# Ids as columns of the first load, bias computed first, base weights of chunk 0 requested ahead of chunk 1

## The chip, the cores and the metric

The kernel runs on one core of a Trainium2 chip. The time is that of the device in microseconds, for one execution. It stands beside the span of a profiled execution, which is the stretch from the first to the last recorded instruction. The engines are PE (TensorE, matrix products), ACT (ScalarE), DVE (VectorE), POOL (GpSimd) and SP (which issues transfers here). PE's weight loads have a row of their own, PEld.

## The reference: a dense layer, two of eight low-rank experts and a residual

`x` has 64 sequences of 32 tokens with 512 features, all in fp32, and each sequence has one id from 0 to 7. Cut to what is computed:

```python
base = einsum('btd,od->bto', x, W)                       # 512 x 512
logits = einsum('btd,ed->bte', x, Wr) + 5.0 * one_hot(id, 8)
topw, topi = top_k(logits, 2)
gates = sum(one_hot(topi, 8) * softmax(topw)[..., None]) # 8 gates for each token, 6 of them zero
h = einsum('btd,erd->bter', x, A)                        # 8 experts, rank 16
lora = einsum('bter,bte,eor->bto', h, gates, B)
out = x + base + 2.0 * lora
```

## The kernel before

**Tiles.** The 2048 tokens make 16 tiles of 128, and partition p holds tokens 16p to 16p + 15, so that each partition belongs to one sequence (two partitions to each of the 64). The 512 features make four chunks of 128 (KC = 4), over which the products sum. A tile has two groups of output columns: *heads*, 392 of them (output columns 256 to 511, the 128 columns of `A`, the 8 logits), and *base*, 256 (output columns 0 to 255). Each group has a PSUM bank for each of three slots, and tile t uses slot t mod 3.

**Three products for one.** For accuracy each fp32 operand is split into a rounded upper part (fp32r) and the rest: `x_hi` and `x_lo`, `w_hi` and `w_lo`, `b_hi` and `b_lo`. A product is then three matmuls, hi by hi (n = 0), `x_hi` by `w_lo` (n = 1) and `x_lo` by `w_hi` (n = 2). ACT makes `x_hi` (L221 for tiles 0 and 1, L231 later), `w_hi` (L224) and `b_hi` (L254). POOL subtracts for `x_lo` (L210, L205). DVE subtracts for `w_lo` (L342) and `b_lo` (L358), and makes `w_hi` of the heads columns of chunk 0 itself (L346).

**The opening.** The host packs the transposed x of tiles 0 and 1 and all the weights into `in_first`, chunk by chunk: 256 columns of x, 392 heads columns, 256 base columns. SP issues x of chunk 0 (L163), then chunks 1, 2 and 3 whole (L165, 452 KB each), then x of tile 2, `b`, and groups of three tiles. ACT issues the heads weights (L242, 196 KB) and then the base weights of chunk 0 (L243, 128 KB). POOL issues the ids (L195), broadcast from 64 numbers to 128 partitions. While these travel, PE runs nine matmuls on constants (L466). Then it goes through tiles 0 and 1 together, chunk by chunk, with a wait in front of each part of a chunk (L469 to L507): for `x_hi`, for `w_hi`, for `x_lo`, for `w_lo`. The last chunk waits for all four and then does heads for both tiles, then base.

**Gates.** As soon as the heads of a tile are done, DVE reads the logits, adds `bias` (L284), finds the two best (L289, L292), builds the gates (L301 to L306, with one exponential on ACT, L239) and writes the gated 128 columns to `gh` (L313). PE transposes `gh` (L424), ACT and DVE split the result (L235, L278), and PE adds its product with `b` into the two banks (`lora`, L433 and L437). DVE adds x and writes the output (L323, L328). For tile 0 the transpose stands on PE behind the first six heads products of tile 2 (L510 to L512).

**Order.** Every engine has its own hand-written order, with semaphores between them. On DVE that of the opening is: cast of the heads weights (L346), `w_lo` of chunk 0's heads, `w_lo` of chunk 0's base and of chunks 1 to 3 (L349 to L351), `bias` (L354, which waits for the ids), `b_lo` (L358), and then the gates of tile 0. On ACT: x of chunk 0, base weights of chunk 0, then x and all weights of each chunk (L248 to L251), x of tile 2, `b`. On POOL: the ids, the identity matrix, the numbers 0 to 7 (`expert`, L198), then `x_lo` of chunks 0 to 3, of tile 2, of tile 3 and so on. Behind tile 3 all engines run loops in steps of one tile.

Of the kernel before, what the change touches and what calls it, by code (L numbers as in the profile page):

```python
# [7 lines left out]
I32 = mybir.dt.int32  # L8
# [22 lines left out]

FIRST = (0, 1)
FIRST_X = len(FIRST) * P
GROUPS = 4
GROUPED = GROUPS * SLOTS


def cond_resid_program(nc: bass.Bass, first: bass.AP, xT: bass.AP, x: bass.AP, ids: bass.AP,
                       b: bass.AP, out: bass.AP):


# [8 lines left out]
    with ctx:  # L50
        def sb(name, shape, dt=FP32):
            return ctx.enter_context(nc.sbuf_tensor(name, shape, dt))
# [4 lines left out]
        def sem(name):  # L57
            return ctx.enter_context(nc.semaphore(name))


        first_sb = sb("first_sb", [P, KC, FIRST_X + WIDTH])
        xT_sb = sb("xT_sb", [P, TILES - len(FIRST), KC * P])
        x_sb = sb("x_sb", [P, TILES, D])
        out_sb = sb("out_sb", [P, TILES, O])
# [2 lines left out]
        b_sb = sb("b_sb", [ER, O])  # L67
        b_hi = sb("b_hi", [ER, O], FP32R)
        b_lo = sb("b_lo", [ER, O], FP32R)
        ids_sb = sb("ids_sb", [P, 1], I32)  # L70
        expert = sb("expert", [P, E], I32)
        bias = sb("bias", [P, E])
        ident = sb("ident", [P, P])
# [30 lines left out]
        wb_landed = sem("wb_landed")  # L104
        chunk_landed = [sem(f"chunk_landed{k}") for k in range(1, KC)]
        b_landed = sem("b_landed")
        ids_landed = sem("ids_landed")
        out_stored = sem("out_stored")

        ident_zeroed = sem("ident_zeroed")  # L110
# [33 lines left out]
        heads_cols, base_cols, all_cols = slice(0, HEADS), slice(HEADS, WIDTH), slice(0, WIDTH)  # L144
        chunks = [slice(k * P, (k + 1) * P) for k in range(KC)]
        first_x = [first_sb[:, k, 0:FIRST_X].rearrange("p (t c) -> p t c", c=P) for k in range(KC)]
        w_sb = first_sb[:, :, FIRST_X:FIRST_X + WIDTH]
        w = first[:, :, FIRST_X:FIRST_X + WIDTH]

        block = ctx.enter_context(nc.Block())  # L150

        @block.sync
        def _(sp):
            def load(dst, src, t, n, landed):
                sp.dma_start(dst[:, bass.ds(t, n), :], src[:, bass.ds(t, n), :]).then_inc(landed, 16)

            def store(t, n):
                sp.dma_start(out[:, bass.ds(t, n), :], out_sb[:, bass.ds(t, n), :]).then_inc(out_stored, 16)

            def load_xT(t, n, landed):  # L160
                load(xT_sb, xT, t - len(FIRST), n, landed)

            sp.dma_start(first_sb[:, 0, 0:FIRST_X], first[:, 0, 0:FIRST_X]).then_inc(x_landed, 16)  # L163
            for k in range(1, KC):
                sp.dma_start(first_sb[:, k, :], first[:, k, :]).then_inc(chunk_landed[k - 1], 16)  # L165
            load_xT(2, 1, xT_third)
            sp.dma_start(b_sb[:, :], b).then_inc(b_landed, 16)
# [12 lines left out]
            with sp.Fori(0, GROUPS) as g:  # L180
                sp.wait_ge(out_made, SLOTS * g + SLOTS)
                store(SLOTS * g, SLOTS)
            for t in range(GROUPED, TILES - 1):
                sp.wait_ge(out_made, t + 1)
                store(t, 1)

            sp.wait_ge(heads_read, TILES)
            sp.dma_start(out[:, TILES - 1, BASE:O], out_sb[:, TILES - 1, BASE:O]).then_inc(out_stored, 16)
            sp.wait_ge(out_made, TILES)
            sp.dma_start(out[:, TILES - 1, 0:BASE], out_sb[:, TILES - 1, 0:BASE]).then_inc(out_stored, 16)  # L190
            sp.wait_ge(out_stored, 16 * (GROUPS + TILES - 1 - GROUPED + 2))

        @block.gpsimd
        def _(pool):
            pool.dma_start(ids_sb[:, :], ids.rearrange("(s a) o -> s a o", a=1)  # L195
                           .to_broadcast([SEQS, P // SEQS, 1])).then_inc(ids_landed, 16)
            nc.gpsimd.memset(ident[:, :], 0.0).then_inc(ident_zeroed, 1)
            nc.gpsimd.iota(expert[:, :], pattern=[[1, E]], base=0, channel_multiplier=0).then_inc(expert_made, 1)  # L198
            pool.wait_ge(ident_zeroed, 1)
            nc.gpsimd.affine_select(out=ident[:, :], in_=ident[:, :], compare_op=ALU.not_equal, fill=1.0, base=0,  # L200
                                    pattern=[[-1, P]], channel_multiplier=1).then_inc(ident_made, 1)

            def x_lower(t, s):
                pool.wait_ge(x_hi_made, t - 1)
                nc.gpsimd.tensor_tensor(x_lo[:, s, :], xT_sb[:, t - len(FIRST), :], x_hi[:, s, :].bitcast(FP32),  # L205
                                        ALU.subtract).then_inc(x_lo_made, 1)

            for k in range(KC):
                pool.wait_ge(chunk_hi_made, k + 1)
                nc.gpsimd.tensor_tensor(x_lo[:, 0:2, chunks[k]], first_x[k],  # L210
                                        x_hi[:, 0:2, chunks[k]].bitcast(FP32), ALU.subtract).then_inc(chunk_lo_made, 1)
            with pool.Fori(0, GROUPS) as g:
                for j in range(2, 2 + SLOTS):
                    x_lower(SLOTS * g + j, j % SLOTS)
            for t in range(2 + GROUPED, TILES):
                x_lower(t, t % SLOTS)

        @block.scalar
        def _(act):
# [3 lines left out]
            def w_upper(k, cols):  # L223
                nc.scalar.activation(w_hi[:, k, cols], w_sb[:, k, cols], ACT.Copy).then_inc(w_hi_made, 1)  # L224
# [15 lines left out]
                                     bias=top[:, 1:2]).then_inc(e2_made, 1)  # L240

            act.dma_start(w_sb[:, 0, heads_cols], w[:, 0, heads_cols]).then_inc(wh_landed, 16)  # L242
            act.dma_start(w_sb[:, 0, base_cols], w[:, 0, base_cols]).then_inc(wb_landed, 16)  # L243
            act.wait_ge(x_landed, 16)
            chunk_upper(0)
            act.wait_ge(wb_landed, 16)
# [1 line left out]
            for k in range(1, KC):  # L248
                act.wait_ge(chunk_landed[k - 1], 16)
                chunk_upper(k)  # L250
                w_upper(k, all_cols)  # L251
            x_upper(2, 2, xT_third, 16)
            act.wait_ge(b_landed, 16)
            nc.scalar.activation(b_hi[:, :], b_sb[:, :], ACT.Copy, scale=SCALING).then_inc(b_hi_made, 1)  # L254
# [20 lines left out]
        def _(dve):  # L275
# [65 lines left out]
            def w_lower(k, cols):  # L341
                nc.vector.tensor_tensor(w_lo[:, k, cols], w_sb[:, k, cols], w_hi[:, k, cols].bitcast(FP32),  # L342
                                        ALU.subtract).then_inc(w_lo_made, 1)

            dve.wait_ge(wh_landed, 16)
            nc.vector.tensor_copy(w_hi[:, 0, heads_cols], w_sb[:, 0, heads_cols]).then_inc(wh_hi_made, 1)  # L346
            dve.wait_ge(wh_hi_made, 1)
            w_lower(0, heads_cols)
            for k in range(KC):  # L349
                dve.wait_ge(w_hi_made, k + 1)  # L350
                w_lower(k, all_cols if k else base_cols)  # L351
            dve.wait_ge(expert_made, 1)
            dve.wait_ge(ids_landed, 16)
            nc.vector.tensor_scalar(bias[:, :], expert[:, :], ids_sb[:, :], LANG_BIAS, ALU.is_equal,  # L354
                                    ALU.mult).then_inc(bias_made, 1)
            dve.wait_ge(bias_made, 1)
            dve.wait_ge(b_hi_made, 1)
            nc.vector.scalar_tensor_tensor(b_lo[:, :], b_sb[:, :], SCALING, b_hi[:, :].bitcast(FP32), ALU.mult,  # L358
                                           ALU.subtract).then_inc(b_lo_made, 1)
# [36 lines left out]
        def _(pe):  # L396
# [7 lines left out]
            def heads_product(s, k, n):  # L404
                return product(heads_ps[s][:, 0:HEADS], s, heads_cols, k, n)
# [67 lines left out]
            pe.wait_ge(w_hi_made, 1)  # L473
            for t in FIRST:
                base_product(t, 0, 0)
            pe.wait_ge(w_lo_made, 1)
            for t in FIRST:
                heads_product(t, 0, 1)
            pe.wait_ge(chunk_lo_made, 1)
            for t in FIRST:  # L480
                heads_product(t, 0, 2)
                base_product(t, 0, 2)
            pe.wait_ge(w_lo_made, 2)
            for t in FIRST:
                base_product(t, 0, 1)
            for k in range(1, KC - 1):
                pe.wait_ge(chunk_hi_made, k + 1)
                pe.wait_ge(w_hi_made, k + 1)
                for t in FIRST:
                    heads_product(t, k, 0)  # L490
                    base_product(t, k, 0)
                pe.wait_ge(chunk_lo_made, k + 1)
                for t in FIRST:
                    heads_product(t, k, 2)
                    base_product(t, k, 2)
                pe.wait_ge(w_lo_made, k + 2)
                for t in FIRST:
                    heads_product(t, k, 1)
                    base_product(t, k, 1)
            pe.wait_ge(chunk_hi_made, KC)  # L500
            pe.wait_ge(w_hi_made, KC)
            pe.wait_ge(chunk_lo_made, KC)
            pe.wait_ge(w_lo_made, KC + 1)
            for t in FIRST:
# [67 lines left out]
```

## Time and profile before

| | us |
|---|---|
| median of 3 runs (lowest, highest) | 82.12 (82.05, 82.36) |
| profiled execution, its own time | 82.09 |
| its span | 80.3 |
| PE busy | 75.4 |
| DVE busy | 50.7 |
| POOL busy | 22.9 |
| ACT busy | 22.4 |

Between the profiled execution's time and its span lie 1.79 us that the profile does not show. PE's granted clock is written as 1.00 in every stretch of the opening. A matmul row is the time from issue to the end that the profile models; successive matmuls overlap, so that the distance between their starts is shorter than a row's length. "idle before" names the time for which the engine had nothing running, and what released it. Later rows of a pipelined engine can begin before the row ahead has ended. A row that waits for something held by another engine can be long without work.

### The profile page before, as it was taken

Reading aid. Unit: us, or ns where it says so; the run is one execution under the profiler, and the core shown is the slowest. Engines: PE = TensorE matmul, PEld = TensorE weight load, DVE = VectorE, ACT = ScalarE, POOL = GpSimd, SP = SyncE. Lnnn points to the kernel's source line nnn. Section 1 sums busy time; section 2 is a strip of 40 time slices with the busy share of each in tenths; the row PEclk is TensorE's granted clock in tenths of the full one; section 3 lists DMA queues with packets and bytes.
Section 4 is the critical chain, followed back from the end, with each engine's and each line's share of the span. In section 5 each row is a group of like instructions: output and inputs, shape, how many; then the busy total and the mean of one; then the engine's idle time right before and its main releaser. Section 6 shows DMA issues by size and latency. Waiting matters only on the chain.

```text
span 80.3 us, 1626 instructions
## 1 busy us (share of the span) xinstructions
PE 75.4 (94%) x505; PEld 70.9 (88%) x505; DVE 50.7 (63%) x216; ACT 22.4 (28%) x56; POOL 22.9 (28%) x26
## 2 busy tenths in 40 slices
PE   6979999699999999999999999999999999999960
PEld 2329889499999999999999999999999999999950
DVE  0075388878778756648292828475573979788670
ACT  1634871135140505031141414050412214111200
POOL 4333482050623060606032321406060604100000
PEclk9999999999999999999999999999999999999999
DMA  1948997489289199999830000080000009032124
GB/s 14 321 162 297 416 426 331 52 321 404 36 263 441 62 269 433 412 249 385 337 141 3 0 0 0 40 352 0 0 0 0 0 0 392 0 131 85 46 105 160
DMA packets 3781, 14.22 MB, mean 177 GB/s; under 512 B 449, under 2 KB 1089, under 8 KB 3521
## 3 DMA queue, kind: packets, MB, share of 16 engines
q1 hardware_dynamic: 3456, 13.84, 46.2%
q10 hardware_dynamic: 288, 0.33, 1.3%
q8 instruction: 2, 0.03, 0.1%
q14 instruction: 3, 0.02, 0.1%
q0 software_dynamic: 32, 0.00, 0.0%
HBM read 9.98 MB, written 4.19 MB: 177 GB/s over the span
## 4 chain that ended last, share of the span: by engine, by line
PE 77%; DMA 9%; DVE 5%; issue 2%; SPq 2%; ACT 1%; DVEq 0%
PE heads_ps L401 36%; PE base_ps L401 25%; DMA first_sb<-in_first 9%; PE base_ps L433 5%; PE heads_ps L433 5%; PE base_ps L437 2%; PE heads_ps L437 2%; PE ghT_ps L424 2%; DVE bias L354 2%; SPq L165 1%; DVE b_lo L358 1%; ACT w_hi L224 1%; DVE out_sb L328 1%; ACT x_hi L221 1%; SPq L163 0%
## 5 line engine op out<-in xcount | busy, mean ns | idle before, releaser
L205 POOL TENSOR_TENSOR x_lo<-xT_sb,x_hi 128x512 fp32r<-128x512 f32 x14 | 18.2, 1301 | 39.5 <-ACT x_hi L231 39.5
L401 PE MATMUL heads_ps<-w_hi,x_hi 128*128 128x392 f32 x64 | 23.3, 369 | 0.1
L401 PE MATMUL heads_ps<-w_hi,x_lo 128*128 128x392 f32 x64 | 21.6, 340 | 0.0
L401 PE MATMUL heads_ps<-w_lo,x_hi 128*128 128x392 f32 x64 | 21.6, 341 | 0.0
L401 PE MATMUL base_ps<-w_hi,x_hi 128*128 128x256 f32 x64 | 18.1, 285 | 0.5 <-ACT w_hi L224 0.5
L401 PE MATMUL base_ps<-w_hi,x_lo 128*128 128x256 f32 x64 | 17.9, 280 | 0.0
L401 PE MATMUL base_ps<-w_lo,x_hi 128*128 128x256 f32 x64 | 17.8, 280 | 0.0
L401 PEld LDWEIGHTS heads_ps<-w_hi,x_hi 128*128 128x128 f32 x64 | 12.2, 192 | 1.6 <-issue 0.6
L401 PEld LDWEIGHTS base_ps<-w_hi,x_hi 128*128 128x128 f32 x64 | 12.0, 188 | 1.1 <-ACT w_hi L224 1.1
L235 ACT ACTIVATE ghT_hi<-ghT_ps 128x128 fp32r<-128x128 f32 x15 | 4.1, 276 | 31.0 <-PE ghT_ps L424 31.0
L278 DVE TENSOR_TENSOR ghT_lo<-ghT_ps,ghT_hi 128x128 fp32r<-128x128 f32 x15 | 4.3, 290 | 13.1 <-ACT ghT_hi L235 13.1
L401 PEld LDWEIGHTS base_ps<-w_hi,x_lo 128*128 128x128 f32 x64 | 12.0, 188 | 0.0
L401 PEld LDWEIGHTS heads_ps<-w_hi,x_lo 128*128 128x128 f32 x64 | 12.0, 188 | 0.0
L401 PEld LDWEIGHTS heads_ps<-w_lo,x_hi 128*128 128x128 f32 x64 | 12.0, 189 | 0.0
L401 PEld LDWEIGHTS base_ps<-w_lo,x_hi 128*128 128x128 f32 x64 | 12.0, 188 | 0.0
L239 ACT ACTIVATE e<-top 128x1 f32<-128x1 f32 x16 | 4.7, 296 | 16.0 <-DVE top L289 16.0
L231 ACT ACTIVATE x_hi<-xT_sb 128x512 fp32r (+1 forms) x14 | 8.7, 621 | 0.4 <-issue 0.4
L323 DVE TENSOR_TENSOR out_sb<-heads_ps,x_sb 128x256 f32 (+1 forms) x16 | 6.7, 418 | 0.7 <-PE heads_ps L437 0.7
L306 DVE SCALAR_TENSOR_TENSOR gate<-expert,top_atf,second 128x8 f32<-128x8 int32 x16 | 6.8, 425 | 0.0
L313 DVE SCALAR_TENSOR_TENSOR gh<-heads_ps,rden,gate 128x128 f32<-128x128 f32 x16 | 5.6, 350 | 1.7
L328 DVE TENSOR_TENSOR out_sb<-base_ps,x_sb 128x256 f32 (+1 forms) x16 | 6.6, 414 | 0.0
L342 DVE TENSOR_TENSOR w_lo<-first_sb,w_hi 128x648 fp32r<-128x648 f32 (+2 forms) x5 | 4.1, 828 | 3.1 <-ACT w_hi L224 3.0
(44 smaller groups left out, 92.5 us busy)
## 6 DMA issues: line engine op xcount, KB each, us to landing
x_sb<-in_x SPq DMA_DIRECT2D x4, 768.0 KB, 5.6
out<-out_sb SPq DMA_DIRECT2D x4, 768.0 KB, 4.0
xT_sb<-in_xT SPq DMA_DIRECT2D x3, 768.0 KB, 4.4
first_sb<-in_first SPq DMA_DIRECT2D x3, 452.0 KB, 6.6
xT_sb<-in_xT SPq DMA_DIRECT2D x1, 1024.0 KB, 6.3
x_sb<-in_x SPq DMA_DIRECT2D x1, 1024.0 KB, 9.7
out<-out_sb SPq DMA_DIRECT2D x3, 256.0 KB, 2.0
xT_sb<-in_xT SPq DMA_DIRECT2D x1, 256.0 KB, 7.4
```

The source lines that it names most:

```text
L205: nc.gpsimd.tensor_tensor(x_lo[:, s, :], xT_sb[:, t - len(FIRST), :], x_hi[:, s, :].bitcast(FP32), ALU.subtract).then_inc(x_lo_made, 1)
L231: nc.scalar.activation(x_hi[:, s, :], xT_sb[:, t - len(FIRST), :], ACT.Copy).then_inc(x_hi_made, 1)
L235: nc.scalar.activation(ghT_hi[s][:, :], src[:, 0:P], ACT.Copy).then_inc(ghT_hi_made, 1)
L239: nc.scalar.activation(e2[:, :], top[:, 0:1], ACT.Exp, scale=-1.0, bias=top[:, 1:2]).then_inc(e2_made, 1)
L278: nc.vector.tensor_tensor(ghT_lo[s][:, :], src[:, 0:P], ghT_hi[s][:, :].bitcast(FP32), ALU.subtract).then_inc(ghT_lo_made, 1)
L306: nc.vector.scalar_tensor_tensor(gate[:, :], expert[:, :], top_atf[:, 0:1], second[:, :], ALU.is_equal, ALU.add).then_inc(gate_made, 1)
L313: nc.vector.scalar_tensor_tensor(gh[s][:, :].rearrange("p (e r) -> p e r", r=R), heads_ps[s][:, REST:REST + ER].rearrange("p (e r) -> p e ...
L323: nc.vector.tensor_tensor(out_sb[:, t, BASE:O], heads_ps[s][:, 0:REST], x_sb[:, t, BASE:O], ALU.add).then_inc(heads_read, 1)
L328: nc.vector.tensor_tensor(out_sb[:, t, 0:BASE], base_ps[s][:, 0:BASE], x_sb[:, t, 0:BASE], ALU.add).then_inc(out_made, 1)
L342: nc.vector.tensor_tensor(w_lo[:, k, cols], w_sb[:, k, cols], w_hi[:, k, cols].bitcast(FP32), ALU.subtract).then_inc(w_lo_made, 1)
L401: return nc.tensor.matmul(dst, xs[:, s, chunks[k]], ws[:, k, cols], start=(k == 0 and n == 0), stop=(k == KC - 1 and n == 2))
L433: nc.tensor.matmul(dst, ghT_hi[s][:, :], bs[:, cols], start=False, stop=False, skip_group_check=True)
```

## The change

The ids become four columns of `in_first` (each partition's id as the bits of a float, repeated; the kernel reads one of them as an int32), between x and the weights. The first transfer, x of chunk 0, takes them along: 260 columns instead of 256. POOL's transfer of the ids and its semaphore go. The other chunks get the same four columns, unused.

The base weights of chunk 0 are issued by SP as its second transfer, ahead of chunks 1 to 3, and no longer by ACT as its second.

On DVE `bias` becomes the first instruction of all; it waits for `expert` and for the first transfer. The wait for `bias_made` between it and `b_lo` goes. On ACT the weights of chunk 1 are rounded in two instructions, heads and then base, and PE's waits count accordingly: the heads products of chunk 1 start on the first, the base products on the second. PE takes the products with `x_lo` of chunk 0 ahead of those with `w_lo`.

```diff
@@ input load
-        first_sb = sb("first_sb", [P, KC, FIRST_X + WIDTH])
+        first_sb = sb("first_sb", [P, KC, FIRST_X + IDS + WIDTH])
-        ids_sb = sb("ids_sb", [P, 1], I32)
+        ids_at = FIRST_X
+        ids_sb = first_sb[:, 0, ids_at:ids_at + 1].bitcast(I32)
@@ SP
-            sp.dma_start(first_sb[:, 0, 0:FIRST_X], first[:, 0, 0:FIRST_X]).then_inc(x_landed, 16)
+            sp.dma_start(first_sb[:, 0, 0:FIRST_X + IDS], first[:, 0, 0:FIRST_X + IDS]).then_inc(x_landed, 16)
+            sp.dma_start(w_sb[:, 0, base_cols], w[:, 0, base_cols]).then_inc(wb_landed, 16)
@@ POOL
-            pool.dma_start(ids_sb[:, :], ids.rearrange("(s a) o -> s a o", a=1)
-                           .to_broadcast([SEQS, P // SEQS, 1])).then_inc(ids_landed, 16)
@@ ACT
-            act.dma_start(w_sb[:, 0, base_cols], w[:, 0, base_cols]).then_inc(wb_landed, 16)
...
-                w_upper(k, all_cols)
+                for cols in ((heads_cols, base_cols) if k == 1 else (all_cols,)):
+                    w_upper(k, cols)
@@ DVE
+            dve.wait_ge(expert_made, 1)
+            dve.wait_ge(x_landed, 16)
+            nc.vector.tensor_scalar(bias[:, :], expert[:, :], ids_sb, LANG_BIAS, ALU.is_equal,
+                                    ALU.mult).then_inc(bias_made, 1)
             dve.wait_ge(wh_landed, 16)
...
-            for k in range(KC):
-                dve.wait_ge(w_hi_made, k + 1)
-                w_lower(k, all_cols if k else base_cols)
-            dve.wait_ge(expert_made, 1)
-            dve.wait_ge(ids_landed, 16)
-            nc.vector.tensor_scalar(bias[:, :], expert[:, :], ids_sb[:, :], LANG_BIAS, ALU.is_equal,
-                                    ALU.mult).then_inc(bias_made, 1)
-            dve.wait_ge(bias_made, 1)
+            dve.wait_ge(w_hi_made, 1)
+            w_lower(0, base_cols)
+            for k in range(1, KC):
+                dve.wait_ge(w_hi_made, k + 2)
+                w_lower(k, all_cols)
@@ PE
-            pe.wait_ge(w_lo_made, 1)
-            for t in FIRST:
-                heads_product(t, 0, 1)
             pe.wait_ge(chunk_lo_made, 1)
             for t in FIRST:
                 heads_product(t, 0, 2)
                 base_product(t, 0, 2)
+            pe.wait_ge(w_lo_made, 1)
+            for t in FIRST:
+                heads_product(t, 0, 1)
...
+                if k == 1:
+                    pe.wait_ge(w_hi_made, 2)
+                    for t in FIRST:
+                        heads_product(t, 1, 0)
+                    pe.wait_ge(w_hi_made, 3)
+                    for t in FIRST:
+                        base_product(t, 1, 0)
```

## Rows read from the trace of the kernel before

**Rows 1.** The page's first part: busy time of PE, its share and instructions.

```profile
PE 75.4 (94%) x505; PEld 70.9 (88%) x505; DVE 50.7 (63%) x216; ACT 22.4 (28%) x56; POOL 22.9 (28%) x26
```

**Rows 2.** Timeline of PE, 4 to 16 us: start, length, instruction, count, idle time before.

```profile
4.43 1.00 PE L401 MATMUL heads_ps<-w_hi,x_hi 128*128 128x392 f32 x2
5.97 0.50 PE L401 MATMUL base_ps<-w_hi,x_hi 128*128 128x256 f32 x2 [0.53 <-ACT w_hi L224]
...
7.51 0.34 PE L401 MATMUL heads_ps<-w_hi,x_hi 128*128 128x392 f32 x1
...
9.18 0.28 PE L401 MATMUL base_ps<-w_lo,x_hi 128*128 128x256 f32 x1
...
11.64 0.42 PE L401 MATMUL heads_ps<-w_hi,x_hi 128*128 128x392 f32 x1
...
14.39 0.34 PE L401 MATMUL heads_ps<-w_hi,x_lo 128*128 128x392 f32 x1
15.48 0.30 PE L424 MATMUL ghT_ps<-ident,gh 128*128 128x128 f32 x1 [0.75 <-DVE gh L313]
```

**Rows 3.** Timeline of DVE, 6 to 14 us.

```profile
6.89 0.84 DVE L342 TENSOR_TENSOR w_lo<-first_sb,w_hi 128x648 fp32r<-128x648 f32 x1 [0.52 <-ACT w_hi L224]
...
10.53 0.97 DVE L342 TENSOR_TENSOR w_lo<-first_sb,w_hi 128x648 fp32r<-128x648 f32 x1 [0.32 <-ACT w_hi L224]
11.42 1.25 DVE L354 TENSOR_SCALAR bias<-expert,ids_sb 128x8 f32<-128x8 int32 x1
12.70 0.69 DVE L358 SCALAR_TENSOR_TENSOR b_lo<-b_sb,b_hi 128x512 fp32r<-128x512 f32 x1
```

**Rows 4.** Timeline of POOL, 6 to 13 us.

```profile
6.30 0.74 POOL L210 TENSOR_TENSOR x_lo<-first_sb,x_hi 128x256 fp32r<-128x256 f32 x1 [1.33 <-ACT x_hi L221]
...
11.20 1.44 POOL L205 TENSOR_TENSOR x_lo<-xT_sb,x_hi 128x512 fp32r<-128x512 f32 x1 [0.39 <-ACT x_hi L231]
```

**Rows 5.** Timeline of DVE and POOL near 17 us and near 24 us.

```profile
16.72 0.23 DVE L306 SCALAR_TENSOR_TENSOR gate<-expert,top_atf,second 128x8 f32<-128x8 int32 x1
...
16.97 1.29 POOL L205 TENSOR_TENSOR x_lo<-xT_sb,x_hi 128x512 fp32r<-128x512 f32 x1 [4.33 <-ACT x_hi L231]
...
23.58 1.28 POOL L205 TENSOR_TENSOR x_lo<-xT_sb,x_hi 128x512 fp32r<-128x512 f32 x1 [2.11 <-ACT x_hi L231]
...
23.68 1.19 DVE L306 SCALAR_TENSOR_TENSOR gate<-expert,top_atf,second 128x8 f32<-128x8 int32 x1
```

**Rows 6.** Timeline of ACT, the rounding of x of chunks 1, 2 and 3.

```profile
5.82 0.40 ACT L221 ACTIVATE x_hi<-first_sb 128x256 fp32r<-128x256 f32 x1
...
8.28 0.42 ACT L221 ACTIVATE x_hi<-first_sb 128x256 fp32r<-128x256 f32 x1 [1.42 <-DMA first_sb<-in_first]
...
9.44 0.42 ACT L221 ACTIVATE x_hi<-first_sb 128x256 fp32r<-128x256 f32 x1
```

**Rows 7.** Two stretches: five engines' busy time, clock, DMA share, GB/s.

```profile
5.00:6.00 1.00, 0.47 (x3) 0.03 (x1) 0.44 (x2) 0.50 (x2) 0.00 (x0) 1.00 0.17 63
7.50:9.00 1.50, 1.50 (x12) 1.50 (x11) 0.23 (x1) 0.72 (x2) 0.22 (x1) 1.00 1.01 401
```

**Rows 8.** Issues: SP's three chunks (start, length); base weights, ids (KB, us to landing).

```profile
1.19 1.38 SPq L165 DMA_DIRECT2D first_sb<-in_first  x3
...
first_sb<-in_first ACTq DMA_DIRECT2D x1, 128.0 KB, 4.3
ids_sb<-in_ids POOLq DMA_DIRECT2D x1, 0.5 KB, 6.0
```

**Rows 9.** Queues' packets: 3.5 to 4.25 (q1, q10), 4.5 to 6, 6 to 7.25 (q0).

```profile
q1 hardware_dynamic: 68, 0.25, 80.2%
q10 hardware_dynamic: 59, 0.06, 22.3%
...
q0 software_dynamic: 6, 0.00, 0.3%
...
q0 software_dynamic: 26, 0.00, 1.6%
```

More of the change, by code:

```diff
@@ L33, with cond_resid_program @@
 FIRST_X = len(FIRST) * P
+IDS = 4
 GROUPS = 4
 GROUPED = GROUPS * SLOTS
-def cond_resid_program(nc: bass.Bass, first: bass.AP, xT: bass.AP, x: bass.AP, ids: bass.AP,
+def cond_resid_program(nc: bass.Bass, first: bass.AP, xT: bass.AP, x: bass.AP,
                        b: bass.AP, out: bass.AP):
@@ L106, in cond_resid_program @@
         b_landed = sem("b_landed")
-        ids_landed = sem("ids_landed")
         out_stored = sem("out_stored")
@@ L146, in cond_resid_program @@
         first_x = [first_sb[:, k, 0:FIRST_X].rearrange("p (t c) -> p t c", c=P) for k in range(KC)]
-        w_sb = first_sb[:, :, FIRST_X:FIRST_X + WIDTH]
-        w = first[:, :, FIRST_X:FIRST_X + WIDTH]
+        ids_at = FIRST_X
+        ids_sb = first_sb[:, 0, ids_at:ids_at + 1].bitcast(I32)
+        w_sb = first_sb[:, :, FIRST_X + IDS:]
+        w = first[:, :, FIRST_X + IDS:]
         block = ctx.enter_context(nc.Block())
@@ L487, in _ @@
                 pe.wait_ge(chunk_hi_made, k + 1)
[L488 to L491, printed above, removed]
+                if k == 1:
[5 more added lines that the diff above has]
+                        base_product(t, 1, 0)
+                else:
+                    pe.wait_ge(w_hi_made, k + 2)
+                    for t in FIRST:
+                        heads_product(t, k, 0)
+                        base_product(t, k, 0)
                 pe.wait_ge(chunk_lo_made, k + 1)
@@ L500, in _ @@
             pe.wait_ge(chunk_hi_made, KC)
-            pe.wait_ge(w_hi_made, KC)
+            pe.wait_ge(w_hi_made, KC + 1)
             pe.wait_ge(chunk_lo_made, KC)
@@ L557 @@
     first_x = xT[:, :ahead].transpose(0, 2, 1, 3).reshape(P, KC, FIRST_X)
+    ids = np.asarray(itok_B_0_7).astype(np.int32).reshape(SEQS).repeat(P // SEQS).view(np.float32)
+    ids = np.broadcast_to(ids.reshape(P, 1, 1), (P, KC, IDS))
     arrays = {
-        "in_first": np.concatenate([first_x, weights], axis=2),
+        "in_first": np.concatenate([first_x, ids, weights], axis=2),
         "in_xT": np.ascontiguousarray(xT[:, ahead:]).reshape(P, TILES - ahead, KC * P),
         "in_x": np.ascontiguousarray(tokens).reshape(P, TILES, D),
-        "in_ids": np.ascontiguousarray(np.asarray(itok_B_0_7).reshape(SEQS, 1)),
         "in_b": np.ascontiguousarray(B.transpose(0, 2, 1)).reshape(ER, O),
```

## The prediction

> **What bounds the kernel now.** The page comes first: PE is busy for 94% of the span [rows 1], and in the chain of waits nearly everything behind 15.48 us is one matmul after the other. So a change in the opening can only move the moment from which PE runs without a break; whatever that moment gains, the end gains, unless a later stall comes in. The timeline of PE then shows where the opening loses time [rows 2]. PE finishes its first two products by the model at 5.43, waits for the rounded base weights until 5.97, and runs chunk 1 from 7.51 to 9.30 (12 matmuls, 1.79 us with the last one's 0.12 us of issue distance). Chunk 3 starts at 11.64, after two waits for data. The last product of tile 2 ahead of the transpose is issued at 14.39 and takes 0.18 us of issue distance, so that PE is ready for the transpose at 14.57, but `gh` is late and it starts at 15.48. That is 0.91 us lost (the row's 0.75 us counts from the modelled end).
>
> Who makes `gh` late is read from DVE's rows [rows 3]. `w_lo` of chunk 3 ends at 11.50, `bias` at 12.67, `b_lo` at 13.39, and the transpose starts 2.09 us behind that, over ten small instructions and their semaphores. `bias` has 128x8 elements and takes 1.25 us, because POOL's `x_lo` of tile 2 [rows 4] is running until 12.64. The two engines exclude each other when both read SBUF. In [rows 3, 4] `w_lo` of chunk 1 is requested at 6.89, POOL's chunk 1 ends at 7.04, and `w_lo` ends 0.69 us behind it. The same instruction `gate` takes 0.23 us alone and 1.19 us under POOL's subtraction, ending with it at 24.87 [rows 5].
>
> Last the transfers. ACT starts chunk 1 at 5.82, straight behind the base weights that landed at 1.19 + 4.3 = 5.49, then sits idle until chunk 2 has landed at 8.28, and has chunk 3 at 9.44 [rows 6, 8]. Chunks 1 to 3 were all issued by 2.57 [rows 8]. In between lies a pause: 63 GB/s and a DMA share of 0.17 from 5 to 6 us, against 401 GB/s from 7.5 to 9 [rows 7]. The software queue has one transfer, the ids. It needs 6.0 us to land [rows 8]. It moves 6 packets in 4.5 to 6 and 26 in 6 to 7.25 [rows 9], which is all it has. With 32 packets on 16 DMA engines these are three engines early and 13 late, and 0.17 of 16 engines is 2.7. The engines that carry chunk 2 through the pause are as many as have the ids behind them; the rest resume with theirs. I read the pause as the price of the ids' transfer. The rows show a coincidence in number and time, not the cause.
>
> **The change, part by part.**
>
> *Ids in the first input.* This removes POOL's DMA of 0.5 KB. It adds 16 bytes to a row of 1024 in the first transfer, 2 KB in 128 KB, which at 401 GB/s is 0.005 us. The reading is worth between nothing (the pause stays) and all of it: 1 us at 63 GB/s instead of 401 is 0.84 us, with its ramps some 1.4 us for chunks 2 and 3. I take it as gone, by the count of engines.
>
> *Base weights of chunk 0 from SP, ahead of chunk 1.* Now they share the DMA engines with chunk 1, and from 3.5 to 4.25 the two queues moved 68 and 59 packets, one for one, though a packet of chunk 1 is 3.6 KB and one of the base weights 1 KB [rows 9]. So they end together, both some 926 KB into the stream. Behind the change 465 KB stand ahead of their end; 461 KB less at 401 GB/s is 1.15 us, so they land at 4.3. PE then rounds on at 5.43 without its wait, and ACT is free when chunk 1 lands, at about 5.5 as the base weights did, instead of 5.82. What it costs: every later issue on SP comes 0.43 us later (1.38 us for three [rows 8]). The first two transfers keep the queue filled meanwhile, and chunk 3 was issued 7 us ahead of its use, so I take nothing; without that cover it is 0.43 us.
>
> *Bias first.* The instruction leaves the stretch 11.42 to 12.67, but what it waited for stays. POOL asks for its `x_lo` of tile 2 from 11.20, gets the port when `w_lo` of chunk 3 lets go, and holds it for 1.14 us (11.50 to 12.64). `b_lo` also reads two SBUF tensors, so it now stands where `bias` stood and ends at 12.64 + 0.54 = 13.18 (0.69 less the 0.15 of start-up that a waiting instruction has behind it, 0.84 against 0.69 for `w_lo`). This saves 0.21 us where the rest stays; if `b_lo` were not held it would save the whole 0.91. I take 0.21. At its new place, as soon as chunk 0 of x has landed, the bias costs DVE up to 0.3 us (a like-sized instruction takes 0.23 [rows 5]) ahead of the cast of the heads weights. PE's warm-up covers most of that; uncovered, it is 0.2 us. If ids arrive later than that cast's input, the cast waits too; both come with the two transfers that are issued first, and I take nothing.
> The Trainium skill, page "SBUF — State Buffer", section "Who interferes with whom", says that a VectorE instruction with two SBUF inputs and a GpSimd one that reads SBUF take an exclusive lock, in order of issue. This trace agrees (1.19 us against 0.23 us). By that rule the early bias alone gives 0.21 us, without it 0.91.
>
> *Chunk 1 rounded in two parts; order of chunk 0's products.* One more ACT instruction, some 0.12 us at ACT's overlap, behind which `w_lo` waits. POOL holds the port until 0.74 us behind its start anyway, so it costs nothing. Without that cover it is 0.12 us. The low part of `x` is used before that of `w`, as POOL's comes first under the lock; nothing on the path. PE's one wait at the end of chunk 3 stays.
>
> *The sum.* With the pause gone, POOL and DVE hand the port back and forth without a gap. From the start s of chunk 1's rounding on ACT: POOL's `x_lo` ends at s + 1.22 (5.82 to 7.04), `w_lo` 0.69 later, `x_lo` of chunk 2 at 0.59 (0.74 less 0.15), `w_lo` 0.69, chunk 3 again 0.59 and 0.69, tile 2's `x_lo` 1.14, `b_lo` 0.54, the transpose 2.09: s + 8.24. With s = 5.5 that is 13.74. Chunk 3 may land as late as 8.3 without harm; without a pause it lands at about 7.5. PE's own chain: chunk 0's products start at 5.43 and take the 1.54 us of 5.97 to 7.51, plus some 0.2 for those at the lower clock (the first two heads products last 1.00 together, 0.50 each, where later ones last 0.34 [rows 2]). Then come 1.79 + 1.79 for chunks 1 and 2, and 2.93 (11.64 to 14.57): 13.7. Both agree, so the transpose starts at 13.75 instead of 15.48. From the profiled execution's 82.09 (span 80.3, 1.79 around it; the runs' median of 82.12 is the same) 1.73 comes off: 80.4. With s = 5.82 and the bias uncovered it is 80.9, and with the tail of chunk 1 landing 0.3 earlier 80.1.
>
> **The rivals.**
>
> *The pause stays* (another cause of it: the ids' packets are then as late as chunk 2 because they share the cause). For it speaks that no ids packet moved before 4.5, as if something held them too; against it, the three engines. Chunks 2 and 3 land as before, and only 0.21 us comes off: 81.9. If in addition chunk 3 follows SP's later issue by 0.43, it is 82.3.
> The Trainium skill, page "DMA: Bandwidth & Descriptors", section "SWDGE vs HWDGE vs iDMA", says that transfers issued from SP or ACT are immune to what holds up GpSimd's descriptors. By that rule the removal frees nothing but itself, and the time is that of this rival; no row shows the descriptors.
>
> *The new order on SP does nothing*: the base weights land no earlier, s stays 5.82, and the sum gives 14.06, or 80.7. The packet counts speak against it.
>
> *Slower: POOL's subtraction of tile 3 overtakes `gate` of tile 1.* Both follow the transpose of tile 0; `gate` starts at 16.72, POOL at 16.97 [rows 5]. If POOL is first, `gate` ends with POOL, about 1.3 us behind its start, and `gh` and the transpose of tile 1 come about 1.0 us late, on PE's path. It decides as soon as `gate` comes 0.25 us later against POOL. With the pause kept that is 82.9. Against it: both hang on the same transpose, and the change touches neither. With the pause gone it would be 81.4.
>
> **How the numbers follow.** The forecast (pause gone, base weights earlier) has 0.58, the order without effect 0.08, the pause that stays 0.24, the slower case 0.10. What a measurement of this kernel can tell from no change is about 0.5%, 0.41 us. So faster has 0.66, the same 0.24, slower 0.10. The forecast's own range is 80.1 to 80.9. As the pause that stays holds 0.24, the range must reach it: 80.1 to 82.3.
>
> **What would show it.** Right: no stretch under 200 GB/s between 3 and 9 us; ACT's chunk 2 starts before 7.1 and chunk 3 before 8.3; `b_lo` still takes over 1 us, ending with 0.54 us behind POOL's tile 2; the transpose of tile 0 at 13.5 to 14.1; from there on PE's rows as before, only shifted. Wrong: a pause near 5 us without any software packets (first rival); base weights on ACT at 5.5 (second); a `gate` over 1 us at tile 1 with PE idle ahead of its transpose (third); or `b_lo` at 0.69 us while POOL subtracts, which would take the lock out of the sum.

## The result: 1.2% faster, a little over half of what was forecast

| | before | after |
|---|---|---|
| median (lowest, highest), us | 82.24 (82.05, 82.46) | 81.28 (80.93, 81.46) |
| profiled execution, its own time, us | 82.09 | 80.93 |
| its span, us | 80.3 | 79.1 |

The ratio is 0.988, with a 95% interval of 0.983 to 0.993: the change takes off 0.96 us (82.24 less 81.28), where 1.73 had been forecast. 81.28 lies outside the forecast's own range of 80.1 to 80.9; it is inside 80.1 to 82.3 only because that range was widened to hold the rival of the pause that stays. The time after varies more than that before, and the profiled execution is the fastest of its four. Ratios here and below compare the faster state of each kernel; an execution more than 1.5% above its kernel's fastest is left out of them.

The page of after, the engines' totals, and the rate of the transfers from 3 to 9 us (the columns are those of [rows 7]):

```profile
PE 74.6 (94%) x505; PEld 70.5 (89%) x505; DVE 51.1 (65%) x216; ACT 22.6 (29%) x57; POOL 22.8 (29%) x25
```

```profile
3.00:9.00 6.00, 5.39 (x30) 4.16 (x29) 3.36 (x6) 3.63 (x9) 2.50 (x4) 1.00 1.03 392
```

The same stretch before moved this much:

```profile
3.00:9.00 6.00, 5.47 (x27) 3.86 (x26) 2.70 (x4) 2.49 (x6) 1.69 (x3) 1.00 0.77 287
```

So the pause of [rows 7] is gone in this execution. Next, the timeline of after: ACT's rounding of the base weights of chunk 0, then of x of chunks 1 to 3.

```profile
4.14 0.42 ACT L224 ACTIVATE w_hi<-first_sb 128x256 fp32r<-128x256 f32 x1
6.08 0.42 ACT L221 ACTIVATE x_hi<-first_sb 128x256 fp32r<-128x256 f32 x1 [1.53 <-DMA first_sb<-in_first]
...
7.26 0.42 ACT L221 ACTIVATE x_hi<-first_sb 128x256 fp32r<-128x256 f32 x1
...
8.40 0.42 ACT L221 ACTIVATE x_hi<-first_sb 128x256 fp32r<-128x256 f32 x1
```

The base weights are there at 4.14, where [rows 8] had them at 5.49. Chunks 2 and 3 are 1.0 us earlier than in [rows 6], though at 7.26 and 8.40 a little behind the 7.1 and 8.3 that the prediction set as its signs. But chunk 1 is later than before, 6.08 against 5.82, and 0.58 later than my 5.5. The timeline of PE, which answers to [rows 2], shows the result:

```profile
4.40 0.64 PE L402 MATMUL heads_ps<-w_hi,x_hi 128*128 128x392 f32 x2
4.88 0.40 PE L402 MATMUL base_ps<-w_hi,x_hi 128*128 128x256 f32 x2
...
7.07 0.59 PE L402 MATMUL heads_ps<-w_hi,x_hi 128*128 128x392 f32 x2 [0.61 <-ACT w_hi L224]
...
13.56 0.34 PE L402 MATMUL heads_ps<-w_hi,x_lo 128*128 128x392 f32 x1
14.45 0.30 PE L425 MATMUL ghT_ps<-ident,gh 128*128 128x128 f32 x1 [0.56 <-DVE gh L313]
```

The wait of 0.53 us for the base weights is gone, and one of 0.61 us for chunk 1 has come in. The transpose of tile 0 starts at 14.45 instead of 15.48, and is still late for PE, which was ready at 13.74. Last DVE and POOL, against [rows 3, 4]:

```profile
3.76 0.23 DVE L347 TENSOR_SCALAR bias<-expert,first_sb 128x8 f32<-128x8 int32 x1 [3.76 <-DMA first_sb<-in_first]
...
10.60 1.77 DVE L359 SCALAR_TENSOR_TENSOR b_lo<-b_sb,b_hi 128x512 fp32r<-128x512 f32 x1
```

```profile
10.16 1.66 POOL L205 TENSOR_TENSOR x_lo<-xT_sb,x_hi 128x512 fp32r<-128x512 f32 x1 [0.17 <-ACT x_hi L231]
```

The bias takes 0.23 us in its new place. `b_lo` takes 1.77 us in its old one and ends at 12.37, 0.55 behind POOL's 11.82: DVE waits for what both engines read SBUF through, which the texts below call the port.

### The profile page after: what moved, and what is told of

Read it like the earlier page. It is cut to its first block, busy times and chain, and to the rows that moved or that the text cites. A ratio compares the mean times of both kernels' runs of the same rounds, so it can differ in the third digit from the quotient of the medians.

```text
span 79.1 us, 1625 instructions
## 1 busy us (share of the span) xinstructions
PE 74.6 (94%) x505; PEld 70.5 (89%) x505; DVE 51.1 (65%) x216; ACT 22.6 (29%) x57; POOL 22.8 (29%) x25
## 3 DMA queue, kind: packets, MB, share of 16 engines
q1 hardware_dynamic: 3600, 13.98, 47.4%
## 4 chain that ended last, share of the span: by engine, by line
PE 78%; DMA 7%; DVE 6%; SPq 2%; ACT 1%; issue 1%; DVEq 0%
PE heads_ps L402 36%; PE base_ps L402 25%; DMA first_sb<-in_first 7%; PE heads_ps L434 5%; PE base_ps L434 5%; PE ghT_ps L425 2%; PE base_ps L438 2%; PE heads_ps L438 2%; DVE b_lo L359 2%; DVE w_lo L342 1%; SPq L167 1%; ACT w_hi L224 1%; SPq L165 1%; DVE out_sb L328 1%; ACT x_hi L221 1%
## 5 line engine op out<-in xcount | busy, mean ns | idle before, releaser
L402 PE MATMUL heads_ps<-w_hi,x_hi 128*128 128x392 f32 x64 | 22.7, 361 | 0.6 <-ACT w_hi L224 0.6
L306 DVE SCALAR_TENSOR_TENSOR gate<-expert,top_atf,second 128x8 f32<-128x8 int32 x16 | 5.8, 364 | 0.0
L301 DVE TENSOR_SCALAR second<-expert,top_atf,e 128x8 f32<-128x8 int32 x16 | 5.7, 357 | 0.0
```

The costliest lines, as they stand in the source:

```text
L301: nc.vector.tensor_scalar(second[:, :], expert[:, :], top_atf[:, 1:2], e2[:, :], ALU.is_equal, ALU.mult).then_inc(second_made, 1)
L306: nc.vector.scalar_tensor_tensor(gate[:, :], expert[:, :], top_atf[:, 0:1], second[:, :], ALU.is_equal, ALU.add).then_inc(gate_made, 1)
L402: return nc.tensor.matmul(dst, xs[:, s, chunks[k]], ws[:, k, cols], start=(k == 0 and n == 0), stop=(k == KC - 1 and n == 2))
```

## The experiments

Two quantities carry all that follows. One is s, the start of chunk 1's rounding on ACT; the other is the start T of the transpose of tile 0. An execution's time less its T was 66.48 in after (80.93 less 14.45) and 66.61 in before (82.09 less 15.48). It lies between 66.3 and 66.9 in every profile below, so what happens behind the transpose matters little. T less s was forecast at 8.24; after has 8.37. "After" and "the changed kernel" are the same. One profile shows one execution of each kernel, and where that is not a usual one the text says so.

**The changed kernel again, and the kernel before without the ids' transfer only.** The first is the measure for all others:

> The changed kernel again, beside the others on the same chip, as their measure. Both theories: a ratio to before of 0.988, some 81.2 us, no pause in the transfers between 3 and 9 us, the transpose of tile 0 near 14.4.

It measured 81.31 us (80.94 to 81.66), ratio 0.988 (0.983 to 0.992). Its profiled execution was the slowest of its four, 81.66, and that shows what varies. Its transfers from 3 to 9 us and at their lowest, then chunk 1 on ACT, then PE:

```profile
3.00:9.00 6.00, 4.65 (x25) 3.40 (x24) 2.70 (x5) 3.01 (x7) 2.03 (x3) 1.00 1.00 349
4.50:5.50 1.00, 1.00 (x7) 1.00 (x8) 1.00 (x2) 0.09 (x1) 0.45 (x1) 1.00 0.81 185
```

```profile
6.81 0.42 ACT L221 ACTIVATE x_hi<-first_sb 128x256 fp32r<-128x256 f32 x1 [2.22 <-DMA first_sb<-in_first]
```

```profile
7.79 0.60 PE L402 MATMUL heads_ps<-w_hi,x_hi 128*128 128x392 f32 x2 [1.32 <-ACT w_hi L224]
...
15.16 0.30 PE L425 MATMUL ghT_ps<-ident,gh 128*128 128x128 f32 x1 [0.54 <-DVE gh L313]
```

A dip to 185 GB/s is back although no ids are transferred, chunk 1 comes 0.73 later than in the other profile, and T is 0.71 later (T less s: 8.35). The expectation of no pause missed here: the changed kernel has a shorter one in a part of its executions. It goes with the order on SP. Two more kernels below have that order and no ids' transfer, with POOL's wait (e4) and with the late bias (e6), and their profiles show 185 and 149 GB/s from 4.5 to 5.5. The five profiles with the base weights on ACT and no ids' transfer (e1, e5, e8, e9, e11) show 387 GB/s or more there.

The second kernel (e1) is before, with this part of the change alone (and the host's packing that belongs to it):

```diff
-            sp.dma_start(first_sb[:, 0, 0:FIRST_X], first[:, 0, 0:FIRST_X]).then_inc(x_landed, 16)
+            sp.dma_start(first_sb[:, 0, 0:FIRST_X + IDS], first[:, 0, 0:FIRST_X + IDS]).then_inc(x_landed, 16)
...
-            pool.dma_start(ids_sb[:, :], ids.rearrange("(s a) o -> s a o", a=1)
-                           .to_broadcast([SEQS, P // SEQS, 1])).then_inc(ids_landed, 16)
...
-            dve.wait_ge(ids_landed, 16)
+            dve.wait_ge(x_landed, 16)
```

> The kernel before with one part of the change: the ids travel as columns of the first transfer, POOL's software transfer is gone; base weights, bias, rounding and order stay as before. Theory A (the software transfer of the ids holds up the DMA engines): no stretch under 200 GB/s between 3 and 9 us, chunk 2 on ACT before 7.3, POOL and DVE hand the port on without a gap, and the transpose of tile 0 comes at s + 8.4 with s near 5.9 to 6.1, so 14.3 to 14.5; about 1.0 us less than before, 81.2. Theory B (the pause has another cause): chunk 2 at 8.3 as before, transpose at 15.5, 82.2.

It measured 80.63 us, ratio 0.981 (0.977 to 0.985): 1.42 us less than before, and 0.7 less than the whole change. Three of its five executions lie between 80.59 and 80.63; the other two took 82.16 and 82.28. Its profile is that of the longest, in which PE's products kept the length of the first ones until about 10 us though the granted clock is written as 1.00, so only the transfers and ACT are read from it:

```profile
3.00:9.00 6.00, 5.38 (x18) 3.82 (x17) 3.75 (x5) 3.83 (x9) 3.13 (x4) 1.00 1.05 410
```

```profile
5.59 0.42 ACT L223 ACTIVATE w_hi<-first_sb 128x256 fp32r<-128x256 f32 x1 [1.49 <-DMA first_sb<-in_first]
5.91 0.40 ACT L220 ACTIVATE x_hi<-first_sb 128x256 fp32r<-128x256 f32 x1
...
6.85 0.40 ACT L220 ACTIVATE x_hi<-first_sb 128x256 fp32r<-128x256 f32 x1
```

There is no pause, chunk 2 is on ACT at 6.85, and s is 5.91. Theory A is confirmed and theory B falls. The gain was even larger than expected. The base weights arrive late, as before, and in the three shorter executions that costs nothing that can be seen; whether PE's wait for them has to do with the two longer ones, no run shows.

**The ids' transfer put back into the changed kernel**, into a tile that nobody reads, on POOL's software queue (e2) and then on ACT's hardware queue (e3):

```diff
+            pool.dma_start(ids_again[:, :], ids.rearrange("(s a) o -> s a o", a=1)
+                           .to_broadcast([SEQS, P // SEQS, 1])).then_inc(ids_landed, 16)
             nc.gpsimd.memset(ident[:, :], 0.0).then_inc(ident_zeroed, 1)
```

> The changed kernel with POOL's old ids transfer put back, into a tile that nobody reads; nothing waits for it before the end. Theory A: the pause near 5 us is back, chunk 2 on ACT at 8 or later, the transpose of tile 0 at 15.2 to 15.4, 82.0 us (before less the 0.2 us of the early bias). Theory B: no pause, as the changed kernel, 81.2.

```diff
             act.dma_start(w_sb[:, 0, heads_cols], w[:, 0, heads_cols]).then_inc(wh_landed, 16)
+            act.dma_start(ids_again[:, :], ids.rearrange("(s a) o -> s a o", a=1)
+                           .to_broadcast([SEQS, P // SEQS, 1])).then_inc(ids_landed, 16)
```

> The changed kernel with the same small ids transfer added on ACT's hardware queue as its second, into a tile that nobody reads. If it is the software queue that stops the engines: no pause, within 0.1 us of the changed kernel. If it is the 4-byte packets on any queue: a pause as in before, 82.0 us.

They measured 82.67 (ratio 1.006, 1.004 to 1.008) and 82.77 us (1.007, 1.005 to 1.009). The transfers of both from 3.5 to 5.5, first POOL's kernel, then ACT's:

```profile
3.50:5.50 2.00, 2.00 (x7) 1.16 (x5) 1.60 (x4) 0.83 (x2) 0.73 (x1) 1.00 0.54 107
```

```profile
3.50:5.50 2.00, 2.00 (x9) 1.28 (x8) 1.71 (x4) 0.83 (x2) 0.73 (x1) 1.00 0.44 75
```

Chunk 1 starts on ACT at 7.62 and 8.65, and T is 15.99 and 17.01 (8.37 and 8.36 behind s). The second profile is that of the longest of eight executions, 83.81 us, so its later s and its lower rate are not to be set against the first's. By the medians, one transfer of 512 bytes costs the changed kernel 1.4 us on POOL's queue and 1.5 on ACT's, more than the 0.8 that was expected. So it is not the software queue that stops the engines. Both kernels are slower than before, for the pause now stands in front of chunk 1 instead of chunk 2. In this execution of the kernel with ACT's transfer SP itself stalls as well; its timeline shows `b` taking 1.61 us to issue, where [rows 8] has 0.46 for one transfer:

```profile
3.08 0.43 SPq L158 DMA_DIRECT2D xT_sb<-in_xT  x1
3.55 1.61 SPq L171 DMA_DIRECT2D b_sb<-in_b  x1
```

**What about the ids' transfer does it?** Both kernels here (e9 and e11) have the base weights on ACT again, as e5 below, and one transfer added behind them on ACT's queue, with 1 KB rows or with 8-byte rows:

```diff
+            act.dma_start(w_again[:, :], w[:, 0, base_cols]).then_inc(again_landed, 16)
```

> e5 with one ordinary transfer more on ACT's queue, the base weights of chunk 0 a second time (128 KB in 1 KB rows), into a tile that nobody reads. If any further transfer in the opening brings the pause: SP's issue instructions grow over 0.5 us, a stretch under 200 GB/s, chunk 1 on ACT a microsecond or more later than 5.6, 81.7 or more. If it is the 4-byte rows of the ids: no such stretch, everything behind it 0.33 us later at most (128 KB at 400 GB/s), 80.7 to 81.0.

```diff
-            act.dma_start(w_again[:, :], w[:, 0, base_cols]).then_inc(again_landed, 16)
+            act.dma_start(w_again[:, :], w[:, 0, 0:2]).then_inc(again_landed, 16)
```

> As e9, but the added transfer on ACT's queue has 128 rows of 8 bytes (two of the weights of each partition) instead of 1 KB, each row read once, into a tile that nobody reads. If short rows alone bring the pause: a stretch under 200 GB/s between 3 and 7 us, SP's issue instructions over 0.5 us, chunk 1 or 2 on ACT a microsecond later than in e9, 81.7 or more. If it needs the ids' own pattern (64 numbers of 4 bytes in one short stretch of memory, each read twice): none of these, 80.6 to 80.8.

They measured 80.73 and 80.79 us (ratios 0.984, 0.982 to 0.985, and 0.986, 0.983 to 0.989). Neither has a pause; the row is that of the kernel with 8-byte rows:

```profile
3.00:9.00 6.00, 5.58 (x28) 4.02 (x27) 3.97 (x7) 4.46 (x11) 3.24 (x4) 1.00 1.04 397
```

So in this place neither one more transfer nor short rows bring the pause. What remains is what only the ids' transfer has: a tensor of its own, 64 neighbouring numbers of 4 bytes, each read twice. Which of these it is stays open. The test is not quite clean: in e3 the added transfer was ACT's second, issued at 1.20, with the base weights on SP, while here it is ACT's third, issued at 1.68. The kernel before had its pause with the base weights on ACT, which speaks against that difference, but the ids' transfer was not tried in this very place.

**The base weights back on ACT's queue** (e5), in the changed kernel:

```diff
             sp.dma_start(first_sb[:, 0, 0:FIRST_X + IDS], first[:, 0, 0:FIRST_X + IDS]).then_inc(x_landed, 16)
-            sp.dma_start(w_sb[:, 0, base_cols], w[:, 0, base_cols]).then_inc(wb_landed, 16)
...
             act.dma_start(w_sb[:, 0, heads_cols], w[:, 0, heads_cols]).then_inc(wh_landed, 16)
+            act.dma_start(w_sb[:, 0, base_cols], w[:, 0, base_cols]).then_inc(wb_landed, 16)
```

> The changed kernel with the base weights of chunk 0 issued by ACT again, as its second transfer. If the order on SP matters: base weights rounded near 5.4 instead of 4.14, PE idle for 0.5 us or more ahead of them; chunk 1 starts on ACT where the base weights let it, 5.7 to 6.1. As POOL and DVE's chain runs from chunk 1, the time is within 0.3 us of the changed kernel. If the order on SP delays chunk 1 (issued 0.43 us later): 0.2 to 0.4 us faster than the changed kernel.

It measured 80.68 us, ratio 0.983 (0.980 to 0.986), 0.6 less than the changed kernel: its four executions (80.56 to 80.85) are all below the eight of the changed kernel (80.93 to 81.66). Its ACT and PE:

```profile
5.30 0.42 ACT L223 ACTIVATE w_hi<-first_sb 128x256 fp32r<-128x256 f32 x1 [1.38 <-DMA first_sb<-in_first]
5.62 0.40 ACT L220 ACTIVATE x_hi<-first_sb 128x256 fp32r<-128x256 f32 x1
```

```profile
5.77 0.50 PE L402 MATMUL base_ps<-w_hi,x_hi 128*128 128x256 f32 x2 [0.58 <-ACT w_hi L223]
...
13.98 0.30 PE L425 MATMUL ghT_ps<-ident,gh 128*128 128x128 f32 x1
```

PE waits 0.58 us for the base weights again, and the kernel is still faster, because chunk 1 starts at 5.62 and T is 13.98. The 0.2 to 0.4 us that had been put on a delay by SP's order were too little, but the direction is that of the second case: the place on SP helps the base weights and hurts chunk 1, and only chunk 1 is on the path. This kernel also has all other parts of the change, and yet its 80.68 is no better than the 80.63 of the ids alone: the 0.2 us of the early bias, read below from T less s, does not show between these two, and why stays open.

**Why is chunk 1 late?** Two kernels ask. In the first (e7), chunks 2 and 3 are issued only when the base weights have landed, so that less traffic follows chunk 1. In the second (e10), SP issues chunk 1 ahead of the base weights.

```diff
             for k in range(1, KC):
+                if k == 2:
+                    sp.wait_ge(wb_landed, 16)
                 sp.dma_start(first_sb[:, k, :], first[:, k, :]).then_inc(chunk_landed[k - 1], 16)
```

> The changed kernel, but SP issues chunks 2 and 3 only when the base weights have landed (near 4.1 us instead of 2.1), so that little traffic follows chunk 1. It asks why chunk 1 started on ACT at 6.08 and not at 5.5. If traffic behind chunk 1 holds up its slowest engine and its completion: ACT starts chunk 1 near 5.5. If it is the amount of data or the later issue of chunk 1: 6.08 again. Chunk 2 lands later by 0.5 to 1 us in both, so the total time is 0 to 0.5 us more than the changed kernel.

```diff
-            sp.dma_start(w_sb[:, 0, base_cols], w[:, 0, base_cols]).then_inc(wb_landed, 16)
             for k in range(1, KC):
                 sp.dma_start(first_sb[:, k, :], first[:, k, :]).then_inc(chunk_landed[k - 1], 16)
+                if k == 1:
+                    sp.dma_start(w_sb[:, 0, base_cols], w[:, 0, base_cols]).then_inc(wb_landed, 16)
```

> The changed kernel, but SP issues chunk 1 ahead of the base weights of chunk 0 (x, chunk 1, base, chunk 2, chunk 3). Chunk 2 is still the fourth transfer on SP, issued at 2.1. If the place of chunk 1 is what costs: chunk 1 rounded on ACT at 5.6 or, behind the base weights, 5.9, and 80.6 to 80.9. If the later issue of chunk 2 brings the dip near 5 us in a part of the runs: a dip under 300 GB/s and a spread of over 0.4 us stay, median 81.0 to 81.5.

The first measured 82.79 us (ratio 1.007, 1.004 to 1.010), more than expected. Its profile is that of the longest execution, 83.8 us: chunk 2 came at 9.93, 2.7 us later than in after, PE waited for it until 11.12, and from 12.5 to 15.5 the granted clock was 0.50 (1.2 of 2.4 GHz). How much of this the others had is not shown. Its chunk 1 answers the question, at 6.19:

```profile
6.19 0.42 ACT L223 ACTIVATE x_hi<-first_sb 128x256 fp32r<-128x256 f32 x1 [1.58 <-DMA first_sb<-in_first]
...
9.93 0.42 ACT L223 ACTIVATE x_hi<-first_sb 128x256 fp32r<-128x256 f32 x1 [2.59 <-DMA first_sb<-in_first]
```

Traffic behind chunk 1 is not what delays it, by this one execution. The second kernel measured 80.94 us, ratio 0.987 (0.985 to 0.988). That is just above the 80.6 to 80.9 expected for the place of chunk 1 and just below the 81.0 to 81.5 of the other case. Its executions but for the profiled one (80.75 to 81.17) overlap those of the changed kernel, and so do the intervals of the ratios, so the time decides nothing. Its profile is that of an execution of 83.87 us, in which the base weights, third on SP, reached ACT only at 7.38 and held up everything, and in which the granted clock was then 0.50 from 9 to 12 us; the others can't have had them so late. Whether the dip is gone in those no profile shows.

But the profiles also have each transfer's time from issue to landing, and there chunk 1 does not depend on when ACT turns to it. Chunk 1 in after, issued third on SP at 1.66, and in e10, issued second at 1.18:

```profile
first_sb<-in_first SPq DMA_DIRECT2D x1, 454.0 KB, 4.4
```

```profile
first_sb<-in_first SPq DMA_DIRECT2D x1, 454.0 KB, 3.7
```

So it landed at 6.06 in after and at 4.9 in e10, where only its place on SP was another. The other profiles without the ids' transfer say the same. With chunk 1 issued second (e1, e5, e8, e9, e11) it took 3.9 to 4.2 us and landed between 5.1 and 5.4; issued third (a0, e4, e6, e7) it took 4.5 to 5.3 us and landed between 6.1 and 7.0. The place on SP is what makes chunk 1 late: 0.48 us by the later issue, the rest by a longer way to landing, whose cause stays open.

**The port.** POOL's subtraction of tile 2 is made to wait for `b_lo`, in the changed kernel (e4) and in the one with the base weights on ACT (e8); and the bias is put back at its old place in the changed kernel (e6).

```diff
+            pool.wait_ge(b_lo_made, 1)
             with pool.Fori(0, GROUPS) as g:
```

> The changed kernel with one wait added: POOL's subtraction of tile 2 waits for b_lo, so that b_lo gets the port behind w_lo of chunk 3. Theory (the port is exclusive and b_lo stands behind POOL's 1.14 us): b_lo takes 0.7 us or less and ends near 11.3 instead of 12.4, POOL's tile 2 ends near 12.6, just ahead of PE's need of it at 12.7 to 13.0, and the transpose of tile 0 is bound by PE at 13.75 to 13.9 instead of 14.45: 0.5 to 0.7 us less than the changed kernel, near 80.6. Rival (b_lo slow for another reason, or POOL's tile 2 becomes late for PE): 0 to 0.3 us less, or up to 0.5 us more.

> Base weights on ACT's queue as in e5 (80.7 us, transpose of tile 0 at 13.98 with PE ready near 13.7), and POOL's subtraction of tile 2 behind b_lo as in e4, where it took 0.25 us off the stretch from chunk 1's rounding to the transpose. Expected: b_lo 0.7 us, POOL's tile 2 ready near 12.6, the transpose bound by PE near 13.7 to 13.8: 80.4 to 80.5. Rival (POOL's tile 2 becomes late for PE by as much as gh gains): 80.7.

The first measured 81.29 us, ratio 0.988 (0.984 to 0.993): no change in the median, where 0.5 to 0.7 us had been expected. Its profile has s at 6.77, so it is read against T less s. DVE, POOL and PE:

```profile
11.29 0.68 DVE L360 SCALAR_TENSOR_TENSOR b_lo<-b_sb,b_hi 128x512 fp32r<-128x512 f32 x1
```

```profile
12.32 1.28 POOL L205 TENSOR_TENSOR x_lo<-xT_sb,x_hi 128x512 fp32r<-128x512 f32 x1 [1.65 <-DVE b_lo L360]
```

```profile
13.76 0.42 PE L403 MATMUL heads_ps<-w_hi,x_hi 128*128 128x392 f32 x1 [0.22 <-POOL x_lo L205]
...
14.91 0.27 PE L426 MATMUL ghT_ps<-ident,gh 128*128 128x128 f32 x1
```

`b_lo` takes 0.68 us instead of 1.77: POOL's instruction is what made it slow. But POOL starts 0.35 us behind the end of `b_lo`, and PE now waits for POOL ahead of tile 2. T less s is 8.14 instead of 8.36: of the 0.7 us by which `gh` was late for PE, 0.2 are gained. The second kernel measured 80.58 us over five executions (80.52 to 80.61), ratio 0.981 (0.980 to 0.983), 0.1 less than without the wait; its T less s is 8.14 too (14.01 less 5.87). It is the best of all that were tried, by an amount at the edge of what the runs can tell.

```diff
-            dve.wait_ge(expert_made, 1)
-            dve.wait_ge(x_landed, 16)
-            nc.vector.tensor_scalar(bias[:, :], expert[:, :], ids_sb, LANG_BIAS, ALU.is_equal,
-                                    ALU.mult).then_inc(bias_made, 1)
             dve.wait_ge(wh_landed, 16)
...
+            dve.wait_ge(expert_made, 1)
+            dve.wait_ge(x_landed, 16)
+            nc.vector.tensor_scalar(bias[:, :], expert[:, :], ids_sb, LANG_BIAS, ALU.is_equal,
+                                    ALU.mult).then_inc(bias_made, 1)
+            dve.wait_ge(bias_made, 1)
             dve.wait_ge(b_hi_made, 1)
```

> The changed kernel with the bias at its old place between w_lo of chunk 3 and b_lo. Theory (lock): the bias takes POOL's 1.1 to 1.7 us, b_lo then its own 0.69, so 0.2 us more than the changed kernel. Rival (no lock on b_lo): 0.9 to 1.2 us more.

It measured 81.64 us (80.9 to 82.26, eight executions), too wide a spread for 0.2 us. The profile tells more, with the same pattern as [rows 3]:

```profile
11.49 1.25 DVE L356 TENSOR_SCALAR bias<-expert,first_sb 128x8 f32<-128x8 int32 x1
12.78 0.69 DVE L360 SCALAR_TENSOR_TENSOR b_lo<-b_sb,b_hi 128x512 fp32r<-128x512 f32 x1
```

With s at 6.98 and T at 15.55, T less s is 8.57, against 8.35 to 8.37 with the bias first. That is 0.2 us for the early bias, as forecast, from one profile of this kernel.

## Why the prediction was right in kind and half off in size

- **The bound.** Right. T moves the end: it came 1.03 earlier in the profiled execution, whose time fell by 1.16; the other 0.13 came behind T.
- **Ids in the first input.** Right, and now by test: without their transfer the pause is gone, with it back it is back. The coincidence of three early engines pointed to the right transfer. The first rival, the pause that stays, falls: chunk 2 came 1.0 us earlier, and the same transfer on ACT's queue costs as much, so it is not what holds up POOL's own transfers. One sign that I had set for it did come, a stretch under 200 GB/s near 5 us without any software packets, in the profile of a0; it belongs to the order on SP, not to the ids. The price was too low: by the sum, the ids alone are worth 1.2 us (5.82 and 8.24, with 0.21 for the late bias, give 14.27 against 15.48), and they measured 1.42.
- **Base weights ahead of chunk 1.** This is the step that failed. I had them land at 4.3 (ACT had them at 4.14), and the removed wait of PE was real. But I took chunk 1 at 5.5, reasoning that the same bytes stand ahead of its end whatever the order. It started at 6.08 and 6.81 in the two profiles. That term is mis-sized by 0.58 to 1.31, and T by 0.70 to 1.41 (14.45 and 15.16 against 13.75). Instead of a gain of 0.32 from this part there is a loss of 0.6: 81.3 against 80.68 with the base weights on ACT. I had priced the later issue of every transfer on SP at nothing, with "without that cover it is 0.43 us", and for chunk 1 there was no cover: it was issued 0.48 later (1.66 against 1.18) and took longer to land, 4.4 to 5.3 us against 3.7 to 4.2. Some executions have the dip near 5 us on top. The count of bytes that I set the landing by fails as well. Adding up the rates of the profile (an estimate), 0.93 MB, all up to the end of chunk 1, had moved by 4.9 us in after, and chunk 1 landed at 6.06. Such a loss was not among the rivals: I had "the new order does nothing" and no rival in which it does harm.
- **Bias first.** Right: 0.2 us by T less s, and the instruction 0.23 us in its new place. No median shows it.
- **The port.** Right. POOL and DVE hand it on, `b_lo` ends 0.55 behind POOL (forecast 0.54), and T less s is 8.37, 8.35, 8.37, 8.36 in four profiles (forecast 8.24).
- **Chunk 1 in two parts, order of chunk 0's products.** Nothing can be told: the ids alone (80.63) and all but the base weights' place (80.68) are the same, though the second has the early bias too.
- **Slower by `gate` and POOL.** It did not happen; no profile of after has a `gate` over 0.25 us at tile 1. That the measured 81.28 is near this rival's 81.4 is chance.

With s put at 6.08 and 6.81 the forecast's own sum gives 14.32 and 15.05, which are 80.9 and 81.7. The two profiled executions took 80.93 and 81.66.

## What to carry to other kernels

A transfer of a few hundred bytes can cost more (here 1.4 us) than one of half a megabyte (1.1 us at the 401 GB/s of [rows 7]): let small inputs ride in a transfer that is needed anyway, and look at the rate of the transfers around its landing before judging it by its size. Before a request is moved ahead of another, ask whose lateness sets the chain that ends last, and read when each transfer landed, not only when its reader began; here the wait that PE showed was covered, and the chunk that was moved back was what DVE and POOL hung on. Where two engines hand a port back and forth, sum their instructions as one chain from its first input, and compare executions by that input.

## What the runs showed of the hardware that I had not expected

- The transfer of 64 ids to 128 partitions, 512 bytes, brought the transfers down to 107 GB/s over 2 us on POOL's queue, and to 75 GB/s on ACT's in a long execution (83.81 us), where 128 rows of 8 bytes from the large input did nothing (397 GB/s from 3 to 9 us). SP's issue of an ordinary transfer took 1.61 us meanwhile in that long execution, instead of 0.43.
- A short transfer can land very late: 128 KB issued third on SP, behind chunk 1, reached ACT only at 7.38 in one execution (of 83.87 us), where as second transfer it was there at 4.14. From issue to landing that is 5.7 us against 2.9.
- A transfer's place on SP's queue counts beyond its later issue: 454 KB took 3.7 to 4.2 us to land as second transfer and 4.4 to 5.3 as third.
- PE's pace rose at different moments. The two first heads products took 1.00 us together before and 0.64 in after, with nothing changed ahead of them, and in one execution of the kernel with the ids alone the heads products still took 0.53 us each at 9.35. Behind a wait of 1.94 us (e7) and one of 2.41 us (e10) the granted clock was 0.50, 1.2 of 2.4 GHz (from 12.5 to 15.5 and from 9 to 12 us), and the same products took 0.53 us instead of 0.34; behind a wait of 3.04 us in e3's profile it stayed at 1.00.
- An instruction that waits for a semaphore on POOL started 0.35 us behind the end of what it waited for (11.97 to 12.32).
